# GpSimd's share of the MLP's low halves and of the residual sums, rearranged against VectorE in a fused attention and MLP kernel

## The reference

```python
def _L0_attn_ref(x, ln1_g, ln1_b, wq, wk, wv, wo, ln2_g, ln2_b, w1, w2):
    x = x + _linear_attention(_layernorm(x, ln1_g, ln1_b), wq, wk, wv, wo)
    h = _layernorm(x, ln2_g, ln2_b)
    x = x + _lookup_act(h @ w1) @ w2        # gelu read at 256 grid points, step 0.1
    return x
...
x = L0_attn_x                               # (2, 4096, 256) float32
x = x + _L0_attn_ref(_layernorm(x, axis=-1), ...)
x = x + _L0_ffn_ref(_layernorm(x, axis=-1), L0_ffn_CB, L0_ffn_SCB, L0_ffn_bias)
                                            # (x @ CB.T) * SCB/127 + bias, 256 to 256
```

## Time and profile before

| | us |
|---|---|
| median of 3 runs | 632.77 (631.15 to 634.07) |
| the profiled execution, device time | 633.82 |
| its span, first to last instruction | 632.0 |
| TensorE busy | 579.8 (92%) |
| VectorE, ScalarE, GpSimd busy | 504.9 (80%), 411.3 (65%), 380.4 (60%) |
| mean granted TensorE clock | 0.979 of full speed |

### The profile page before, as it was taken

One profiled execution on the slowest core, in us unless ns is written; L12 is line 12 of the kernel. 1 busy time (PEld: TensorE's weight loads), 2 busy tenths in 40 slices (PEclk: granted clock), 3 DMA queues, 4 the chain that ended last, 5 costly groups with the idle time before them and its releaser, 6 DMA issues.

```text
span 632.0 us, 12211 instructions
## 1 busy us (share of the span) xinstructions
PE 579.8 (92%) x3838; PEld 514.7 (81%) x3838; DVE 504.9 (80%) x1076; ACT 411.3 (65%) x767; POOL 380.4 (60%) x337
## 2 busy tenths in 40 slices
PE   6999999999997999999999999999999999999894
PEld 5788778878786888889888897888978889788684
DVE  5688988898874688879887798877988779887555
ACT  2467767676665875866758676586765857658560
POOL 3536464655442448585585856858567585675752
PEclk8799999999998999999999999999999999999898
DMA  8111112010101000110101101011010110100001
GB/s 285 65 45 56 66 33 66 33 66 35 68 1 52 2 33 34 33 66 0 66 27 39 67 1 66 20 47 66 0 66 11 55 66 0 66 6 29 34 1 68
DMA packets 11128, 29.16 MB, mean 46 GB/s; under 512 B 2016, under 2 KB 4576, under 8 KB 11104
## 3 DMA queue, kind: packets, MB, share of 16 engines
q1 hardware_dynamic: 9472, 28.32, 12.4%
q10 hardware_dynamic: 1632, 0.53, 0.4%
HBM read 20.45 MB, written 8.39 MB: 46 GB/s over the span
## 4 chain that ended last, share of the span: by engine, by line
PE 37%; DVE 23%; POOL 17%; issue 15%; ACT 5%; DMA 1%; DVEq 1%; POOLq 0%; ACTq 0%; SPq 0%
PE psum L914 32%; PE psum L932 5%; DVE f32r_arena L738 4%; POOL f_arena L351 3%; DVE bn_stats L615 3%; POOL f32r_arena L343 3%; DVE f_arena L657 3%; POOL f_arena L372 3%; POOL f_arena L367 2%; DVE f_arena L729 2%; DVE f_arena L642 2%; POOL f_arena L336 2%; DVE f32r_arena L768 2%; POOL rstd L324 2%; DVE f_arena L755 1%
## 5 line engine op out<-in xcount | busy, mean ns | idle before, releaser
L914 PE MATMUL psum<-w_hi,f32r_arena 128*128 128x256 f32 x1280 | 179.5, 288 | 22.8 <-DVE f32r_arena L738 16.9
L914 PEld LDWEIGHTS psum<-w_hi,f32r_arena 128*128 128x128 f32 x1280 | 165.6, 191 | 36.1 <-issue 20.5
L540 ACT ACTIVATE grid_index<-psum,w_bias_in_steps 128x512 int8<-128x512 f32 x128 | 87.1, 680 | 95.3 <-PE psum L914 95.3
L914 PE MATMUL psum<-f32r_arena,w_hi 128*128 128x512 f32 x512 | 141.6, 408 | 4.6 <-issue 4.0
L914 PE MATMUL psum<-f32r_arena 128*128 128x512 f32 (+1 forms) x512 | 121.3, 380 | 2.1 <-issue 1.5
L914 PEld LDWEIGHTS psum<-f32r_arena,w_hi 128*128 128x128 f32 x512 | 89.6, 191 | 23.3 <-ACT grid_index L540 5.5
L343 POOL TENSOR_TENSOR f32r_arena<-f_arena,f32r_arena 128x512 fp32r<-128x512 f32 x64 | 83.0, 1297 | 35.9 <-ACT f32r_arena L550 35.4
L914 PEld LDWEIGHTS psum<-f32r_arena 128*128 128x128 f32 x512 | 83.9, 192 | 14.2 <-issue 2.7
L729 DVE TENSOR_SCALAR f_arena<-f_arena,mean_var,rstd 128x256 f32<-128x256 f32 x124 | 71.2, 634 | 25.7 <-POOL rstd L324 25.7
L548 ACT ACTIVATE f_arena<-grid_index 128x512 f32<-128x512 int8 x128 | 81.0, 633 | 7.0 <-DVE f32r_arena L738 0.4
L550 ACT ACTIVATE f32r_arena<-grid_index 128x512 fp32r<-128x512 int8 x128 | 79.3, 619 | 0.0
(11 more groups left out here) (96 smaller groups left out, 957.4 us busy)
## 6 DMA issues: line engine op xcount, KB each, us to landing
f_arena<-in_L_attn_x_dram SPq DMA_DIRECT2D x32, 512.0 KB, 3.3
out_dram<-f_arena SPq DMA_DIRECT2D x15, 512.0 KB, 2.6
f_arena<-in_L_attn_w_dram SPq DMA_DIRECT2D x2, 1024.0 KB, 11.0
out_dram<-f_arena SPq DMA_DIRECT2D x2, 256.0 KB, 2.8
phi_q<-in_L_attn_wk_dram ACTq DMA_DIRECT2D x1, 256.0 KB, 5.0
phi_q<-in_L_attn_wv_dram ACTq DMA_DIRECT2D x1, 256.0 KB, 5.5
phi_q<-in_L_attn_wq_dram SPq DMA_DIRECT2D x1, 256.0 KB, 5.8
phi_q<-in_L_ffn_CB_dram SPq DMA_DIRECT2D x1, 256.0 KB, 7.8
```

The source lines that it names most:

```text
L540: act(k8[:, m % 2], bank(AB + m % 2), ACT.Identity, scale=1.0 / STEP, bias=h_bias[:, m:m + 1]).then_inc(s["grid_ready"], 1)
L914: return nc.tensor.matmul(out_, lhs, rhs, start=start, stop=stop, skip_group_check=True)
```

## The change

GpSimd and VectorE swap two of the eight low halves: low(0) moves from GpSimd to VectorE, low(7) from VectorE to GpSimd. VectorE then has m = 0, 1, 3, 5 and GpSimd 2, 4, 6, 7; `low_done` gives semaphore and count for block m, and ScalarE and TensorE wait by it.

On GpSimd two waits are added: before low(2) for norm 3 being done on VectorE (n3_ready), before low(4) for norm 2 (n2_ready). The sum xb = xp + bias moves from behind GpSimd's first LayerNorm to the place between low(2) and pow 2. low(7) stands behind the first LayerNorm and ahead of the last sum.

On VectorE the mean and variance of chunk i - 1 move ahead of low(0) and attn_low, and y2 with its statistics moves ahead of low(3).

```diff
+        LOW_V, LOW_P = (0, 1, 3, 5), (2, 4, 6, 7)
+        def low_done(c, m):
+            on_v = m in LOW_V
+            return s["t_lo_v" if on_v else "t_lo_p"], c * (MT // 2) + (LOW_V if on_v else LOW_P).index(m) + 1
...
# GpSimd's body
                     nc.gpsimd.tensor_tensor(xz, x2[p], y2, ALU.add).then_inc(s["xz_ready"], 1)
-                    mlp_low(i, 0)
                 if prv:
                     power(i - 1, u3, r3, mv3, "mv3_ready", "u3_ready", "pow3")
                 if main:
+                    if prv:
+                        g.wait_ge(s["n3_ready"], i)
                     mlp_low(i, 2)
-                if nxt:
-                    power(i + 1, u2, r2, mv2, "mv2_ready", "u2_ready", "pow2")
-                if main:
-                    mlp_low(i, 4)
-                if main:
-                    mlp_low(i, 6)
-                if nn:
-                    first_norm(i + 2, p, turn + 1)
                 if prv:
                     wait(g, stored, i * 16)
                     nc.gpsimd.tensor_tensor(tm(xb), tm(xp), bias_b.unsqueeze(1).to_broadcast([P, TT, D]),
                                             ALU.add).then_inc(s["xb_ready"], 1)
+                if nxt:
+                    power(i + 1, u2, r2, mv2, "mv2_ready", "u2_ready", "pow2")
+                if main:
+                    if nxt:
+                        g.wait_ge(s["n2_ready"], i + 2)
+                    mlp_low(i, 4)
+                    mlp_low(i, 6)
+                if nn:
+                    first_norm(i + 2, p, turn + 1)
+                if main:
+                    mlp_low(i, 7)
...
# VectorE's body
                     sums(xp, bn_b, "bn3")
+                    mean_var(i - 1, bn_b, mv3, "bn3", "mv3_ready")
+                if main:
+                    mlp_low(i, 0)
                 if nxt:
                     attn_low(i + 1)
-                if prv:
-                    mean_var(i - 1, bn_b, mv3, "bn3", "mv3_ready")
...
                     normalise(i - 1, xp, mv3, r3, "pow3", "n3_ready")
+                if nxt:
+                    first_residual(i + 1)
                 if main:
                     mlp_low(i, 3)
-                if nxt:
-                    first_residual(i + 1)
...
                     attend(i + 2, 0)
-                if main:
-                    mlp_low(i, 7)
                 if nn:
                     attend(i + 2, 1)
...
# TensorE, down(m); ScalarE's gelu(m) waits by low_done(c, m - 2) in the same way
-                    pe.wait_ge(s["t_lo_p" if m % 2 == 0 else "t_lo_v"], c * (MT // 2) + (m // 2 + 1))
+                    pe.wait_ge(*low_done(c, m))
```

More of the change, by code:

```diff
@@ L545, in gelu @@
                 a.wait_ge(s["grid_ready"], n + 3)
-                wait(a, s["t_lo_p" if m % 2 == 0 else "t_lo_v"], c * (MT // 2) + m // 2)
+                if m > 1:
+                    a.wait_ge(*low_done(c, m - 2))
+                elif not is_chunk(c, 0):
+                    a.wait_ge(*low_done(c - 1, m + MT - 2))
                 act(tf[m % 2], k8[:, m % 2], ACT.Gelu_apprx_tanh, scale=STEP)
```

## The result

| | before | after |
|---|---|---|
| median (range) of 4 runs, us | 633.42 (631.15 to 634.49) | 612.89 (611.49 to 617.22) |
| profiled execution, its span, us | 633.82, 632.0 | 617.22, 615.5 |
| mean granted TensorE clock | 0.979 | 0.976 |
| us per body, xp to xp, bodies 1 to 13 | 26.42 | 25.0 |

The ratio is 0.97 (95% interval 0.9672 to 0.9727), 20.5 us less. The forecast was 612.0 with a range of 604 to 625. Two further profiles of the same kernel have spans of 611.2 and 610.2 us; the forecast's span was 610.8.

The account below looks back on a forecast made before the run. TensorE was taken to bound a body up to some two us of standing still, caused by the other engines' chain. 1.0 - 19.7 - 1.4 - 0.8 - 0.3 = -21.2 us gave a median of 611.6, said as 612, range 604 to 625.

Parts of the forecast that it names:

- The body, 24.9: Loop of phase 2, one xp to the next: 24.9 us instead of 26.42, 1.5 us less.
- What decides the next xp: End of a body: by down(7) xp would come at 24.70, by attend half 1 at 24.9; the later decides.
- Down(7) and low(7): Late in a body: low(7) ends 23.32 us after xp's start, down(7) starts at 23.38 instead of 25.01; gain 1.63 us.
- more than 0.7: Sign that the forecast is wrong: ScalarE waiting for low(4) by more than 0.7 us.
- Body 0: First body: low(4) waits for norm 2, low(6) for low(4), low(7) follows the first LayerNorm; loses 1.0 us (0 to 1.5).
- The clock in bodies 14 and 15: After body 14's wait, now about 1.6 us, the lower clock costs less: between nothing and 1.6 us, half taken, -0.8.
- GpSimd taking the turn: Rival behind xz: pow 3 goes before low(0), which ends at 5.6; 26.3 us a body, about 630; chance 0.08.
- the second rival: Contention not relieved as counted: norm 2 stays 2.3 us or other operations slow; 25.8 a body, 618 to 627; chance 0.15.
- TensorE alone as the bound: Rival in the loop: the chain is shorter than counted; 24.4 us a body, 605 us; chance 0.17.
- The store: Rival: xb waits for the previous chunk's store, delaying pow 2 and the chain; 647 if it lands at 12; chance 0.04.
- the swap does nothing: Rival: low(7) behind the first LayerNorm is as late as before, another 1.6 us; 632 us; chance 0.05.
- 0.51 us a body: Start of a body: low(0) and attn_low end earlier, the o product starts at 5.52 instead of 6.03, TensorE 0.51 us ahead.

Follow-up runs that it names:

- The split of the LayerNorm: Changed kernel with GpSimd's first LayerNorm split: scale copied behind xz, two of four instructions ahead of low(6); 612.87 us, ratio 0.9649.

## Why the prediction was right, point by point

**The body, 24.9.** Right in size (24.97) and nearly row by row; no step is over 0.25 us off, and they drift late by 0.1 to 0.2 from low(4) on. Low(0) ended 0.55 us behind xz, as low(7) did behind the sum before; the norms fell to 1.38 us, where the forecast had 1.36. By the Trainium skill (SBUF — State Buffer, Who interferes with whom) issue order decides who blocks, and at the tie behind xz the trace agrees: low(0), issued at T 3.11, ended at T 4.24, and the first instruction of pow 3, at T 3.79, took 0.52 us instead of 0.20 and ended 0.07 behind it.

The prediction said that passes with one operand do not stand still for GpSimd, and in the next sentence that the normalisation does. The normalisation reads one tensor, from SBUF, so the first is too wide: the traces show it only for the statistics (1.41 us beside xz, as elsewhere) and for passes that read PSUM.

**What decides the next xp.** The forecast had attend half 1, with down(7) 0.2 us in front. Measured, they meet: den starts at 452.69 and attend's product ends with xp's start at 453.98, and down(7)'s start plus 1.32 is 453.96. The split of the LayerNorm gave GpSimd 1.4 us to spare and left the body at 24.98. That attend, low(7) and TensorE's own steps all meet here within some 0.2 us was forecast in part (0.1 us at down(7), and attend behind both), but no run shows that attend alone decides. With TensorE busy for 321.91 of 323 us there is little left for any of them to give back in the loop's present order.

**Down(7) and low(7).** ScalarE's wait for low(4) is 0.64 us on average (8.3 over 13), 0.9 at the longest; the text had called more than 0.7 a sign against. On average it stays below, in line with low(4) 0.2 us later than forecast.

**Body 0, mis-sized**: +1.6, forecast +1.0 with 0 to 1.5. Most of the miss is a turn between the two engines that was not counted. VectorE, then GpSimd's low(4) in body 0:

```profile
219.10 0.69 DVE L754 TENSOR_TENSOR f32r_arena<-f_arena,f32r_arena 128x512 fp32r<-128x512 f32 x1
```

```profile
219.27 1.67 POOL L350 TENSOR_TENSOR f32r_arena<-f_arena,f32r_arena 128x512 fp32r<-128x512 f32 x1 [1.57 <-DVE f_arena L745]
```

Low(4), let go by norm 2, starts when VectorE's low(5) is under way, and takes 1.67 us instead of 1.29. That is 0.38 of the 0.6 us that were missing. The loss as a whole comes from the wait for norm 2: from down(0) of body 0 to xp it is 18.6 us before, 20.0 after, and 18.6 again without the two waits.

**The clock in bodies 14 and 15, mis-sized the other way.** Half of 1.6 us was taken; the fall of the clock behind body 14's wait did not come at all (granted clock 1.00 from 577 to 595 us). TensorE's rows where the earlier trace rows had 2.58 us of idle time:

```profile
577.53 1.20 PE L929 MATMUL psum<-w_hi,f32r_arena 128*128 128x256 f32 x8 [1.34 <-POOL f32r_arena L350]
```

The 8 matmuls take 1.20 us (before 1.94), and the idle time is 1.34 where I had said 1.6: of body 14's 2.2 us, 1.24 are the shorter wait and 0.74 these matmuls. With body 14 at -2.2 (forecast -1.4) and the rest at -1.6 (forecast -0.8 and -0.3), the ends gave 1.3 us more than the sum; body 0 took back 0.6.

**The sum.** Loop -18.1 in the first profile (forecast -19.7), since before's 26.42 became 25.02 and not 24.9. The two later spans, 611.2 and 610.2, lie on both sides of the forecast 610.8. That they come so close is in part luck: the loop's shortfall of 1.6 us and body 0's 0.6 are covered by the 1.3 that the ends gave too much, and the start of phase 2 varies between executions by more than any of these.

**The rivals.** GpSimd taking the turn did not happen; forced, it gives 640 and not 630: 13 x (26.69 - 26.3) = 5 us more in the loop, and 3.7 us behind it (65.1 us from xp of body 14 to the end, in after 61.4), which the rival had at nothing. What the second rival named did not come: the norms take 1.38 us and the statistics 1.41. The contention was moved as well as relieved, for low(0) and low(5) still stand still, which the forecast had for low(0) only; and norm 2 at 2.38 us, in the kernel without the waits, cost nothing, where that rival had 0.9 us a body for it (with low(4) waiting). TensorE alone as the bound (24.4 a body) did not come. The store was never in the way: the sum with the bias started as soon as low(2) was done (437.85). That the swap does nothing is refuted for low(7), which costs 19 us back on VectorE. Low(0) was not moved back by itself, nor were mean and variance: what these two parts give (the forecast had 0.51 us a body for them) is argued from the table of T and not shown by a run.

**What the prediction did not see** is how little of the change can be left out; of the parts that were tried, only the two waits can. Against the kernel before: swap alone +17 us, waits alone +15, all but the sum's or y2's new place +11 each, all of it together -20. In three of these four a 2.4 us sum of GpSimd lies over most of a subtraction of VectorE, which then takes 2.27 to 2.80 us; in the fourth, the waits alone, GpSimd's queue reaches xz late. Where the sum with the bias stands behind low(7), xp waits for it as well.

## What to carry to other kernels

Plan the long GpSimd operations by which VectorE passes they lie beside: put them beside passes that read PSUM or beside statistics, and keep VectorE's two-operand SBUF subtractions out of their time, because here a 0.7 us one then ended 0.55 us after GpSimd's and took up to 2.89 us. Then ask of each relief whether the chain that sets the time runs through it: norm 2 was relieved by about 1 us a body, and the kernel without that relief was as fast. When one operation is moved, list what it leaves alone and also what it now lies beside; the edits that failed here took one collision away and made another. A part that looks harmless on its own (a wait, a swap of two halves) can cost 2% in the wrong order, so parts of such a change are to be tried together as well as one by one.

## What the runs showed of the hardware

- The end of a blocked subtraction is 0.55 us behind the GpSimd operation's end in every case read: low(0) and low(5) after the change, low(0) in the swap alone, low(3) with y2 late, low(7) back on VectorE, low(3) with xz behind pow 3.
- It is not only VectorE that loses. GpSimd's low(4) took 1.67 us instead of 1.29 when VectorE's subtraction had begun first.
- Behind 1.34 us of idle TensorE at the end of body 14 the granted clock stayed at 1.00; before, behind 2.58 us at the same place, it was 0.73 over 590 to 594 us. With 1.7 us of idle time ahead of one step in every body the loop was granted 0.98 on average (swap alone, sum with the bias late); with 1.3 and 1.6 us (low(0) waiting for pow 3, low(7) back on VectorE) it kept 1.00.
- The start of phase 2 varies between executions of the same kernel: xp of body 1 at 228.78 and at 224.8, xz of body 0 at 200.38 and at 196.93. The granted clock was below 1.00 at this start in both: 0.57 and 0.58 over 200 to 204 and 204 to 208 us in the one, 0.50 and 0.65 over 196 to 200 and 200 to 204 in the other.
